# Graph layer with experts: edge sums in transposed form, one-hots of 64 nodes, scaled on VectorE

## The reference, cut to what matters

```python
x0, x1 = node[:, :64], node[:, 64:].reshape(N, 64, 3)          # node = layernorm(x)
h0 = x0 @ W_lin1_0 * z / 8;  h1 = einsum('nuc,uv->nvc', x1, W_lin1_1) * z / 8
hid = silu(edge_len @ fc_w0 / sqrt(8))                         # 50000 x 64
wA, wB, wC, wD = split(hid @ fc_w1 / sqrt(64), 4)              # 50000 x 64 each
xs0, xs1 = h0[src], h1[src]                                    # gathered rows of 256 floats
sh0, sh1 = edge_attr[:, :1], edge_attr[:, 1:4]
midA = wA * xs0 * sh0;            midD = wD * einsum('euc,ec->eu', xs1, sh1) / sqrt(3)
midB = (wB * xs0)[:, :, None] * sh1[:, None, :];  midC = wC[:, :, None] * xs1 * sh0[:, None, :]
y0 = segment_sum(concat(midA, midD), dst);  y1 = segment_sum(concat(midB, midC), dst)
out = c_s * self_part + c_x * (y @ W_lin2) * z;   x = x + out;   x = x + experts(layernorm(x))
```

## Time and profile before

| | |
|---|---|
| median of 3 runs | 1334.03 us (1311.8 to 1337.46) |
| span of the profiled execution | 1334.0 us, mean granted clock 0.955 |
| its own time beside the span | 1334.03 us, the median run |
| busy share: PE, PEld, DVE, ACT, POOL | 91%, 84%, 77%, 62%, 54% |
| node block, edge block, update block | to 65.5 us, to 684 us, to some 780 us |

### The profile page before, as it was taken

The page is one execution under the profiler, slowest core; times in us unless marked ns, Lnnn a source line. Parts: engine busy times, 40 slices in busy tenths (PEclk is TensorE's granted clock), DMA queues, the critical chain, the costliest instruction groups (busy, mean ns, idle before and its releaser), DMA issues. The chain is left out here.

```text
span 1334.0 us, 32063 instructions
## 1 busy us (share of the span) xinstructions
PE 1217.9 (91%) x8631; PEld 1120.6 (84%) x8632; DVE 1029.3 (77%) x2584; ACT 826.6 (62%) x2362; POOL 720.3 (54%) x823
## 2 busy tenths in 40 slices
PE   2789999999999999999989899998998997989995
PEld 2578888888888888888887679998998997989995
DVE  7589999999999999999856866444765674666663
ACT  2688888888888888888834674453442443343431
POOL 7178888788887888878731104651242232233332
PEclk9989999999999999999975979999999998999998
DMA  6443444344344444434543474764324334332232
GB/s 241 155 131 111 120 117 119 111 119 120 111 122 120 115 116 118 121 110 118 171 126 116 163 259 131 251 216 140 99 44 103 78 62 99 95 95 46 46 49 28
DMA packets 107219, 160.47 MB, mean 120 GB/s; under 512 B 16414, under 2 KB 82750, under 8 KB 106656
## 3 DMA queue, kind: packets, MB, share of 16 engines
q1 hardware_dynamic: 73680, 90.86, 21.4%
q0 software_dynamic: 29568, 65.62, 20.6%
q10 hardware_dynamic: 3920, 3.41, 0.8%
HBM read 110.99 MB, written 48.85 MB: 120 GB/s over the span
## 5 line engine op out<-in xcount | busy, mean ns | idle before, releaser
L576 ACT ACTIVATE hots<-hot,sh_st 128x128 f32<-128x128 f32 x1568 | 467.9, 390 | 3.8 <-PE psY L743 3.3
L552 POOL DMA_INDIRECT rows<-h_tab,src_st x392 | 404.9, 1033 | 117.2 <-issue 116.9
L743 PEld LDWEIGHTS psY<-prod,hots 128*128 128x128 f32 x2352 | 324.6, 192 | 20.4
L743 PE MATMUL psY<-prod,hots 128*128 128x128 f32 x2352 | 326.1, 275 | 0.0
L1739 POOL DMA_INDIRECT out_rows<-q_ob,q_index x58 | 125.5, 2163 | 294.4 <-DVE q_ob L1837 193.3
L740 PE MATMUL psY<-prod,hots 128*128 128x256 f32 x784 | 234.4, 381 | 0.6 <-DVE prod L636 0.6
L636 DVE TENSOR_TENSOR prod<-psW,rows 128x384 f32<-128x384 f32 x392 | 213.8, 545 | 0.0
L1763 ACT ACTIVATE q_hf<-q_psA,q_b 128x256 f32<-128x256 f32 x232 | 109.7, 473 | 111.7 <-PE q_psA L1293 109.0
L1300 PE MATMUL q_psB<-x_whi,q_hhi 128*128 128x256 f32 x464 | 138.7, 299 | 24.5 <-DVE q_hlo L1815 24.5
L651 DVE TENSOR_TENSOR y_sb<-y_sb,psY 64x512 f32 x196 | 133.4, 681 | 10.2 <-issue 5.7
L1293 PE MATMUL q_psA<-q_xhi,x_whi 128*128 128x256 f32 x464 | 133.2, 287 | 4.0 <-DVE q_xlo L1804 2.8
(11 more groups left out here) (213 smaller groups left out, 2509.6 us busy)
## 6 DMA issues: line engine op xcount, KB each, us to landing
x_raw<-in_w SPq DMA_DIRECT2D x18, 1024.0 KB, 8.0
slots_d<-blank SPq DMA_DIRECT2D x49, 258.0 KB
x_slot_tile<-slots_d SPq DMA_DIRECT2D x30, 258.0 KB, 2.8
s_row<-xn_d SPq DMA_DIRECT2D x50, 128.0 KB, 3.1
cols_lo<-ele_split SPq DMA_DIRECT2D x196, 32.0 KB
rows<-h_tab,src_st POOLq DMA_INDIRECT x392, 2.8
x_sb<-in_x SPq DMA_DIRECT2D x5, 640.0 KB, 5.8
h_tab<-x_sb ACTq DMA_DIRECT2D x5, 640.0 KB, 3.3
```

The lines of the kernel that those rows point to most:

```text
L552: pool.indirect_dma_start(out=rows[p][:, c, :, :].rearrange("p a u -> p (a u)"), out_offset=None, in_=h_tab, in_offset=bass.IndirectOffset ...
L576: ins = nc.scalar.activation(hots[p][:, 4 * c + k, :], hot[p][:, c, :], ACT.Copy, scale=sh_st[p][:, 4 * c + k:4 * c + k + 1])
L743: ins = nc.tensor.matmul(y[:, 2 * k::6 - 2 * k, :][:, 0:2, :], hots[p][:, 4 * c + k + 1, :], a[:, 0::k + 1, :][:, 0:2, :], start=False, st ...
```

## The change

**Edges.** A step's sums are now made transposed: the products are stationary (128 edges x 128 product columns), the scaled one-hots move, and they are 64 node columns wide (`SPAN`), counted from the step's first node. Five regions (`REG`) of 128 x 64 are summed per step, four chunks each: 20 f32 matmuls of 64 columns. The sums lie in `yT` as [128, 5, nodes], and `add_y` is one addition of 128 x 5 x 64. The scaled one-hots are made by VectorE in one multiplication of 128 x 1024 elements (`scale_hot`); ScalarE has only `silu` left. The products of a step are made by four multiplications over all four chunks (768, 256, 768 and 512 elements a partition). The f32r split is gone: `hidden` is one f32 matmul of 256 columns with 16 rows, `radial` is four f32 matmuls of 256 columns with 64 rows each, alternately of the lower and the upper 64 partitions, and into two banks in turn. The gathers take their indices straight from `src_sb`, are unrolled over the 98 steps, and run through a ring of 7 buffers; `sh_st` comes by a transfer on SyncE's queue.

**Node block.** The split of `ele_t` and its round trip through DRAM are gone; the cleared tile is `yT`, 16320 elements a partition in place of 13312.

**Update block.** Staging, transposes and copies of the sums are gone. `mix` takes slices of `yT` as stationary and makes five f32 matmuls of 128 columns per tile. Its weights `w2` are cleared by GpSimd and then loaded by ten transfers in place of five.

```diff
@@ edge_block, gpsimd
-                        pool.wait_ge(prod_done, (r * T + t) * C + C)
-                        pool.tensor_copy(src_st[p][:], src_sb[:, at(t), :] ...).then_inc(src_staged, 1)
-                        pool.wait_ge(hots_done, r * T + t + 1)
-                        pool.tensor_copy(sh_st[p][:], sh_sb[:, at(t), :] ...).then_inc(sh_staged, 1)
+                for t in range(T):
+                    pool.wait_ge(prod_done, (r * T + t) * 2 + 2)
+                    pool.sem_inc(gather_turn, 1)
+                    for c in range(C):
+                        pool.indirect_dma_start(
+                            out=rows[t % RING][:, c, :, :].rearrange("p a u -> p (a u)"), out_offset=None, in_=h_tab,
+                            in_offset=bass.IndirectOffsetOnAxis(ap=src_sb[:, t, c:c + 1], axis=0),
+                        ).then_inc(row_in[t % RING], 16)
@@ edge_block, sync
-                            sp.dma_start(e_st[p][32 * half:32 * half + 2 * NB, :].bitcast(F32),
-                                         ele_split[:, at(first_edge, STEP)]).then_inc(e_in[p], 16)
+                            sp.dma_start(e_st[p][NB * half:NB * (half + 1), :],
+                                         ele_t[:, at(first_edge + PART * half, PART)]).then_inc(e_in[p], 16)
+                        sp.wait_ge(hots_done, r * T + t + 1)
+                        sp.dma_start(sh_st[p][:], sh_t[:, at(first_sh, 4 * C)]).then_inc(sh_in[p], 16)
@@ edge_block, scalar
-                for c in range(C):
-                    for k in range(4):
-                        ins = nc.scalar.activation(hots[p][:, 4 * c + k, :], hot[p][:, c, :], ACT.Copy,
-                                                   scale=sh_st[p][:, 4 * c + k:4 * c + k + 1])
@@ edge_block, vector
-            def high(r, j, p):
-                nc.vector.tensor_copy(hidT[p], hid[p][:]).then_inc(round_done, 1)
-            def low(r, j, p):
-                nc.vector.tensor_tensor(hidT[p][MUL:P, :], hid[p][MUL:P, :], hidT[p][MUL:P, :].bitcast(F32),
-                                        ALU.subtract).then_inc(low_done, 1)
+            def scale_hot(r, use, j, p):
+                dve.wait_ge(sh_in[p], 16 * (r * (T // 2) + use + 1))
+                dve.wait_ge(hot_done, r * T + j + 1)
+                dve.wait_ge(seg_done, r * T + j + 1)
+                nc.vector.tensor_tensor(hots[p][:], hot[p][:].unsqueeze(2).to_broadcast([P, C, 4, SPAN]),
+                                        sh_st[p][:].rearrange("p (c n) -> p c n", c=C).unsqueeze(3)
+                                        .to_broadcast([P, C, 4, SPAN]), ALU.mult).then_inc(hots_done, 1)
 ...
+                nc.vector.tensor_tensor(out_p[:, :, 1:4, :], w[:, :, 2:3, :].to_broadcast([P, C, 3, MUL]),
+                                        x[:, :, 1:4, :], ALU.mult)
+                nc.vector.tensor_tensor(out_p[:, :, 0, :], w[:, :, 0, :], x[:, :, 0, :], ALU.mult).then_inc(prod_done, 1)
+                nc.vector.tensor_tensor(out_p[:, :, 4::2, :], w[:, :, 3:4, :].to_broadcast([P, C, 3, MUL]),
+                                        x[:, :, 1:4, :], ALU.mult)
+                nc.vector.tensor_tensor(out_p[:, :, 5::2, :], w[:, :, 1:2, :].to_broadcast([P, C, 2, MUL]),
+                                        x[:, :, 0:1, :].to_broadcast([P, C, 2, MUL]), ALU.mult).then_inc(prod_done, 1)
 ...
-                for lo, tile in ((0, low_tile), (HALF, high_tile)):
-                    acc = y_sb[lo:lo + HALF, at(tile), :, :].rearrange("p o a u -> p (o a u)")
-                    ins = nc.vector.tensor_tensor(acc, acc, psY[p][lo:lo + HALF, :], ALU.add)
+                acc = yT[:, :, at(low, SPAN)]
+                nc.vector.tensor_tensor(acc, acc, psY[p][:, 0:REG * SPAN].rearrange("p (g n) -> p g n", g=REG), ALU.add
+                                        ).then_inc(y_done, 1)
 ...
+                def turn_of(r, k, q, last=False):
+                    j = k * TURN + 2 + q
+                    add_y(r, j - 2, q % 2)
+                    if not last:
+                        one_hot(r, j + 1, (q + 1) % 2)
+                    products(r, k * 2 + (2 + q) // RING, j, q % 2, (2 + q) % RING)
+                    scale_hot(r, k * RING + 1 + q // 2, j, q % 2)
@@ edge_block, tensor
-                nc.tensor.matmul(psE[:], w0[:], e_st[p], start=True, stop=True).then_inc(hid_done, 1)
+                nc.tensor.matmul(psE[p][:, 0:PART], w0[:], e_st[p][:], start=True, stop=True
+                                 ).then_inc(hid_done, 1)
 ...
-                for c in range(C):
-                    nc.tensor.matmul(o, hidT[p][:, P * c:P * c + P], w1hi[:], start=True, stop=False)
-                    ins = nc.tensor.matmul(o, hidT[p][:, P * c:P * c + P], w1lo[:], start=False, stop=True)
+                for c in (0, 2, 1, 3):
+                    part = slice(MUL * (c // 2), MUL * (c // 2) + MUL)
+                    ins = nc.tensor.matmul(psW[p][:, c, :, :],
+                                           hid[p][part, P * (c % 2):P * (c % 2) + P],
+                                           fc_w[part, :, :], start=True, stop=True)
 ...
+                for c in range(C):
+                    for g in range(2):
+                        nc.tensor.matmul(y[:, g, :], prod[p][:, c, 2 * g:2 * g + 2, :].rearrange("p a u -> p (a u)"),
+                                         hots[p][:, c, 0, :], start=(c == 0 and g == 0), stop=(c == C - 1),
+                                         skip_group_check=True)
+                for c in range(C):
+                    for n, first in enumerate((4, 5, 7)):
+                        ins = nc.tensor.matmul(y[:, 2 + n, :],
+                                               prod[p][:, c, first:first + 2, :].rearrange("p a u -> p (a u)"),
+                                               hots[p][:, c, n + 1, :], start=False, stop=(c == C - 1),
+                                               skip_group_check=True)
@@ update_block
+            sp.wait_ge(wzero, 1)
+            for part, g, n, block_w in ((top, 0, 0, w_a), (bottom, 0, 1, w_c), ...):
+                sp.dma_start(w2[part, g, n, :], block_w).then_inc(w_in, 16)
 ...
-                for c in range(4):
-                    ins = nc.tensor.transpose(psY[i][:, P * c:P * c + P], ys[:, j, P * c:P * c + P], ident[:])
 ...
+                for g_ in range(REG):
+                    cols = (o[:, 0:2, :], o[:, 2:4, :], o[:, 0:2, :], o[:, 0::2, :], o[:, 0::3, :])[g_]
+                    ins = nc.tensor.matmul(cols, yT[:, g_, P * t:P * t + P], w2[:, g_, :, :], start=(g_ == 0),
+                                           stop=(g_ == REG - 1), skip_group_check=True)
```

More of the change, by code:

```diff
@@ L680, in _ @@
+                step(nc.vector.tensor_copy(low_row[:], row_t[:]))
+                step(nc.vector.tensor_scalar(window[:], window[:], float(SPAN), None, ALU.add))
                 one_hot(r, 0, 0)
-                low(r, 0, 0)
-                high(r, 1, 1)
                 one_hot(r, 1, 1)
-                low(r, 1, 1)
-                products(r, 0, 0, 0)
-                high(r, 2, 0)
+                products(r, 0, 0, 0, 0)
+                scale_hot(r, 0, 0, 0)
                 one_hot(r, 2, 0)
-                low(r, 2, 0)
@@ L689, in _ @@
-                products(r, 0, 1, 1)
-                with dve.Fori(0, T // 2 - 2) as k:
-                    for q in range(2):
-                        t = k * 2 + 1 + q
-                        add_y(r, t - 1, q)
-                        high(r, t + 2, 1 - q)
-                        one_hot(r, t + 2, 1 - q)
-                        low(r, t + 2, 1 - q)
-                        products(r, k + 1, t + 1, q)
-                add_y(r, T - 4, 0)
-                high(r, T - 1, 1)
-                one_hot(r, T - 1, 1)
@@ L706, in _ @@
+                with dve.Fori(0, T // TURN - 1) as k:
+                    for q in range(TURN):
+                        turn_of(r, k, q)
+                for q in range(TURN - 2):
+                    turn_of(r, T // TURN - 1, q, q == TURN - 3)
                 add_y(r, T - 2, 0)
@@ L802, in update_block @@
         xlo = [v["cols_lo"], sb("u_xlo1", [P, KC, SH], F32R)]
-        psY = [pb(f"u_psY{i}") for i in range(2)]
         psO = [pb(f"u_psO{i}") for i in range(2)]
@@ L1111, in last_scores @@
                 turn_scores(g, q, GROUP - 1)
-            turn(0, 0, 0)
+            pe.wait_ge(w_ready, 1)
             for j in range(GROUP):
-                if j + 1 < GROUP:
-                    turn(0, 0, j + 1)
-                if j == 0:
-                    pe.wait_ge(w_ready, 1)
                 mix(0, 0, j)
-            with pe.Fori(0, NG // 2) as h:
-                for q in range(2):
-                    b = h * 2 + q
-                    turn(b + 1, 1 - q, 0)
-                    for j in range(GROUP):
-                        if j + 1 < GROUP:
-                            turn(b + 1, 1 - q, j + 1)
-                        mix(b + 1, 1 - q, j)
-                        columns(b, q, j)
```

(7 more changed lines are left out.)

311 lines of the change are left out of this document (103 added, 208 removed).

## The result

The changed kernel takes 1878.49 us (median of four runs, 1874.85 to 1882.31), the kernel before 1331.99 beside it (1311.8 to 1337.46): 1.4218 times as long, with a 95% interval of 1.4096 to 1.4341. The profiled execution took 1878.69 us, its span is 1876.7. The forecast was 1309, its range ended at 1388. The time is that of rival 3, 1900 us at a chance of 0.05.

The account below looks back on a forecast made before the run. VectorE was taken to bound the kernel before, TensorE close behind; after the change TensorE would, at 6.06 us a step. From 1334.0 us, -10 for the steps and -15 for the rest gave 1309 us, range 1278 to 1388.

Parts of the forecast that it names:

- rival 3: Edge block: the clock stays at 0.50, a step takes 12.1 us, +590 if it lasts, 1900 us; chance 0.05.
- Start of the edge block: Edge block's start: one step at half clock and a longer fill, +7 us, bounds 0 to +25.
- VectorE at 4.5 us: Edge step: VectorE's work falls to 4.5 us in place of 6.16, behind TensorE.
- `segment` at 4.25: Edge step, TensorE: 40 pairs of weight load and 64-column matmul take 4.25 us, from 4.2 to 4.5.
- `hidden` at 0.43: Edge step, TensorE: one f32 matmul of 256 columns is two pairs at 0.215, 0.43 us.
- `radial` at 1.08: Edge step, TensorE: eight 256-column pairs take five slots, 1.08 us, as the array's halves run side by side.
- Rival 1: Edge step: the array's halves do not overlap, `radial` takes 1.72, a step 6.70, +53, 1372 us; chance 0.27.
- Changes of shape at 0.1 each: Edge step, TensorE: three changes of the array's shape cost 0.1 us each, 0.3 together, bounds 0.1 to 0.5.
- Sum 6.29 in place of 6.06: Edge step: TensorE's terms sum to 6.06 us against 6.16 before, -10 us over 98 steps.
- The rest was -15: Everything outside the edge steps' pace: node block, edge block's start and end, and update block together -15 us.
- The node block: Node block: a longer clearing costs +2.5, a wait that goes gives -6.4; sum -4 us, bounds -6 to +2.
- The update block: Update block: fewer pairs and waits, later `w2`, a clock that may rise early; together -14 us, bounds -20 to +3.

Follow-up runs that it names:

- the warm start: Changed kernel, loop untouched, plus 22 f32 matmuls of 256 columns on constants around the first `hidden` and `radial`, results unused: 1339.61 us, 1.0224 of the kernel before.

## Why the prediction was wrong

**The step that failed** is the third rival: "`hidden` and `radial`, 256 columns each, speak against it: with such work the clock rose at 78". They did not raise it. The reading was right, the step from it was not. What ran in the kernel before when the clock rose:

```profile
77.50:78.00 0.50, 0.50 (x5) 0.50 (x4) 0.50 (x3) 0.50 (x3) 0.25 (x1) 0.50 0.42 82
78.20:78.40 0.20, 0.20 (x3) 0.20 (x3) 0.20 (x2) 0.20 (x2) 0.20 (x1) 1.00 0.40 144
```

```profile
78.18 0.28 PE L728 MATMUL psW<-w1hi,cols_hi 128*128 128x256 f32 x1
...
78.42 0.59 PE L740 MATMUL psY<-prod,hots 128*128 128x256 f32 x2
```

From 74.01 us to 78.42 TensorE had only `radial` and one `hidden`, one behind the other, and the clock was up before the first `segment`. The prediction took that stretch for what a whole step with such work in it would do. In the changed kernel `hidden` and `radial` are 3.16 of the 11.88 us of a step, the other 8.72 are 64-column pairs, and in 98 steps this mix did not raise the clock. Nor is it their new shapes: in the kernel before with 64 columns the old `radial` and `hidden` ran alone from 74.70 to 79.29, narrow pairs followed, and the clock stayed at 0.50 until 166.

A warning stood in the same group: from 690 to 730 us TensorE was busy 37.87 of 40 us and had 0.50. The prediction set the 1.00 between 730 and 766 against it. But a tile there has 8 pairs of 64 columns among 19, a step of the changed kernel 40 among 50, so that row says little of this mix. And raising and holding differ: with the warm start the same loop holds 1.00 for 600 us, and without it it does not reach it in 1150 (80 to 1230 us, busy all the time). The price of the rival, 12.1 us a step and 1900 us, was right (11.88 and 1878.49); its chance was not. "Start of the edge block", +7 for one step at half clock, was the same error in the sum: it took for granted that the clock would rise.

The Trainium skill's page "TensorE: Matmul & The Clock Gate", section "Why this matters for your kernels", advises to keep TensorE continuously busy and without idle gaps. Here it was busy 400.00 of 400 us and stayed at 0.50, so that advice alone is not enough; the measurement decides.

**The rest of the sum, with the clock up** (the run with the warm start, span 1332.2 against 1334.0, -2 where the forecast was -25). Both spans are single executions, and the kernel before took anything from 1304 to 1341 us, so the parts below say more than their sum; beside each other the medians were 1339.61 and 1328.68.

- VectorE at 4.5 us: 149.22 busy us in 200, so 4.7 a step. Right; it waits for TensorE, as forecast.
- `segment` at 4.25: 1.83 + 2.77 = 4.60, less one change of shape 4.50. The 12 matmuls of L666 have pairs of 0.115, not 0.105. "I take 4.25, near the row of the same shape": eight pairs were too few to choose the low end by; the other end, 4.5, was right. 64 and 96 columns cost the same, so halving the columns buys nothing, as was said.
- `hidden` at 0.43: 0.62 less 0.1 for the shape, 0.52. On 128 rows it is 0.53 less 0.1, the 0.43 of the prediction; its rows were of 128, and 16 rows are 0.09 dearer.
- `radial` at 1.08: 1.07 less 0.1, 0.97. The number was near, the reason wrong. It rested on the halves of the array running side by side in turn; in blocks they take the same 1.07 (2.02 at half clock). A pair on 64 rows is simply cheaper, 0.12 where 128 rows take 0.22. Rival 1 priced the opposite of a thing that decides nothing. The rule on row groups that the prediction took from the Trainium skill (the same page, section "Part 3: Packing small matmuls — row/col tiling") is shown by none of these runs, since neither the order nor the half that comes first changed anything.
- Changes of shape at 0.1 each: right, by the run with `radial` on 128 rows.
- Sum 6.29 in place of 6.06: +13 us over 98 steps where -10 was forecast, against 6.16.
- The rest was -15, and -2 less +13 is -15 as well, but by luck: its parts were off and cancelled. The node block is 5.7 us shorter, forecast -4. The edge block is 12.8 longer (59.7 to 691.0, where it was 65.5 to 684.0), which is the steps' +13, so its start and end together give nothing where +3 was forecast. The update block, up to the first matmul of the experts, takes 87.8 us (691.0 to 778.8) in place of 95.3: -7.5 where -14 was forecast. `w2` comes late as forecast (9.3 us after the block's start in the changed kernel, 4.5 before). The expert blocks give 1.2, for which the forecast had nothing. The edge block's last pairs and the experts' first matmul:

```profile
687.28 2.84 PE L666 MATMUL psY<-hots,prod 128*128 128x64 f32 x24
...
778.78 0.61 PE L1189 MATMUL s_psA<-cols_hi,x_whi 128*128 128x320 f32 x1 [0.70 <-ACTq L1357]
```

In the changed kernel itself the clock did rise early in the update block (0.82 between 1245 and 1250), as the term for it said.

## What to carry to other kernels

Before narrowing the moving operand of an f32 matmul, ask not only what a pair costs at the clock of now, but what exactly ran when the clock rose in this profile. A stretch in which one part of the mix ran alone, as `radial` did before 78.42 us, or in which the clock was merely held, says nothing of the whole mix, and a busy TensorE is no sign of it. Where weight loads set the pace, columns are free up to their length (64 and 96 cost the same 0.115 us here), so fill them: wider moving operands with fewer stationary ones (16 in place of 20 here) gave both the clock and 0.43 us a step. And a term that decides needs more than eight pairs of one row behind it when its bounds are 6% apart.

## What was unexpected of the hardware

- TensorE without a gap for 1150 us at a granted clock of 0.50, and 540 us less when every matmul of the sum moved 32 useless columns more.
- The same loop held 1.00 for 600 us after a warm start, and stayed at 0.50 after the gaps from 77 us on.
- f32 pairs of 256 columns: 0.22 us on 128 rows, 0.12 on 64, whichever half of the array and in whatever order; `hidden` is cheaper with zeros up to 64 rows (with `radial` 1.48) than on 16 (1.69), and a step with 128 rows is as short as with 64 (5.68 and 5.66).
- In eight of the runs the kernel before beside them took 1428.6 or 1432.31 us and TensorE stopped for 0.4 to 2.5 us before single matmuls, in 82 to 128 us above all. TensorE-bound versions lost more there (1.064 of the kernel before in place of 0.984). Its cause is open.
